# The attention output product written beside the scores, behind the products with v, and another order of VectorE's work in a round

## The reference

```python
qkv = x @ Wqkv.T + bqkv                      # x: the layernorm of the input
scores = einsum('bhid,bhjd->bhij', q, k) / sqrt(8)
mask = (j <= i) & (j >= i - 31)
probs = softmax(where(mask, scores, -inf))
y = einsum('bhij,bhjd->bhid', probs, v)
out = y @ Wo.T + bo                          # added to the input
```

## Time and profile before

| | us |
|---|---|
| median of 3 runs (2181.7 to 2184.13) | 2182.03 |
| the profiled execution | 2180.72 |
| its span, first to last instruction | 2178.9 |
| TensorE's matmuls busy in the span | 2027.5 |
| VectorE busy | 1491.8 |
| GpSimd busy | 1439.8 |
| ScalarE busy | 1192.3 |

### The profile page before, as it was taken

The page is one execution under the profiler, slowest core; times in us unless marked ns, Lnnn a source line. Parts: engine busy times, 40 slices in busy tenths (PEclk is TensorE's granted clock), DMA queues, the critical chain, the costliest instruction groups (busy, mean ns, idle before and its releaser), DMA issues. The chain is left out here.

```text
span 2178.9 us, 42631 instructions
## 1 busy us (share of the span) xinstructions
PE 2027.5 (93%) x14462; PEld 1546.1 (71%) x14463; DVE 1491.8 (68%) x2745; ACT 1192.3 (55%) x2383; POOL 1439.8 (66%) x972
## 2 busy tenths in 40 slices
PE   7998999999999988889998888898779999999998
PEld 5776546999999635556665555665554489999994
DVE  6777585333333479999999999999975833333335
ACT  5665323222222269999999988989833232222222
POOL 6775003777767339999999998989940057777660
PEclk9999999999999999999999999989899999999999
DMA  8000100000000423322232222333233000000004
GB/s 301 1 0 2 39 1 13 26 25 24 25 24 25 114 76 98 99 97 99 101 98 93 96 97 89 99 94 94 89 134 145 0 21 26 25 25 25 24 23 120
DMA packets 72343, 141.93 MB, mean 65 GB/s; under 512 B 9979, under 2 KB 43773, under 8 KB 70054
## 3 DMA queue, kind: packets, MB, share of 16 engines
q1 hardware_dynamic: 63142, 121.87, 17.1%
q0 software_dynamic: 9088, 18.63, 2.9%
HBM read 123.82 MB, written 16.65 MB: 64 GB/s over the span
## 5 line engine op out<-in xcount | busy, mean ns | idle before, releaser
L2205 POOL TENSOR_TENSOR m_seen<-m_state,experts 128x1024 f32<-128x1024 f32 x256 | 599.7, 2365 | 58.8 <-DVE m_state L2259 52.2
L2259 DVE TENSOR_TENSOR_SCAN m_state<-experts,ps 128x512 f32<-128x512 f32 x448 | 540.3, 1235 | 1.4 <-PE ps L1796 1.1
L1813 PE MATMUL ps<-ident,m_seen 128*128 128x128 f32 x2048 | 280.0, 282 | 36.9 <-POOL m_seen L2205 36.9
L1813 PEld LDWEIGHTS ps<-ident,m_seen 128*128 128x128 f32 x2048 | 243.7, 145 | 76.0 <-POOL m_seen L2205 56.1
L2018 ACT ACTIVATE experts<-delta,experts 128x512 f32<-128x512 f32 x448 | 291.3, 713 | 1.0 <-DVE delta L2285 0.5
L1527 POOL COPY f_weights<-experts 128x1898 f32 x142 | 252.3, 1777 | 23.9 <-issue 23.5
L1350 PE MATMUL first_up_ps<-f_xT,f_weights 128*128 128x128 f32 x1988 | 241.5, 275 | 1.5 <-issue 1.4
L1350 PE MATMUL ps<-zu,f_weights 128*128 128x128 f32 x1988 | 241.5, 275 | 1.5 <-issue 1.4
L1350 PEld LDWEIGHTS first_up_ps<-f_xT,f_weights 128*128 128x128 f32 x1988 | 233.2, 192 | 2.6 <-issue 2.6
L1350 PEld LDWEIGHTS ps<-zu,f_weights 128*128 128x128 f32 x1988 | 233.2, 192 | 2.6 <-issue 2.6
L2239 DVE TENSOR_TENSOR ps<-m_delta_u,ps 128x512 f32<-128x512 f32 x286 | 193.2, 676 | 12.6 <-PE ps L1771 11.9
(11 more groups left out here) (421 smaller groups left out, 3919.2 us busy)
## 6 DMA issues: line engine op xcount, KB each, us to landing
experts<-m_rows SPq DMA_DIRECT2D x144, 512.0 KB, 3.7
experts<-in_experts SPq DMA_DIRECT2D x17, 1461.0 KB, 18.6
tokens<-f_rows SPq DMA_DIRECT2D x8, 512.0 KB, 4.4
f_rows<-expert_out SPq DMA_DIRECT2D x8, 512.0 KB, 7.0
f_cols<-expert_out SPq DMA_DIRECT2D x8, 512.0 KB, 7.3
out<-X SPq DMA_DIRECT2D x4, 512.0 KB, 3.2
X<-in_x SPq DMA_DIRECT2D x4, 448.0 KB, 6.1
f_xin<-tokens,f_take POOLq DMA_INDIRECT x71
```

The source lines that it names most:

```text
L1813: mm = pe.matmul(Y[:, i // 2, at:at + P], seen[:, n % SEEN, h, i * P:(i + 1) * P], ident[:], is_transpose=True, start=(n == 0 and at == 0) ...
L2205: pool.tensor_tensor(seen[:, n % SEEN], state[:, n % RING], c_rep[:, Q % C_RING, n % C_GROUP, :].unsqueeze(1).to_broadcast([P, HALF, SEG]) ...
L2259: dve.tensor_tensor_scan(state[:, n % RING, h, :], decay_, drive_, before_, ALU.mult, ALU.add).then_inc(s_state, 1)
```

## The change

- The output product is written to `beside_scores`: columns 256 to 383 of the second of the four score banks, one block of 128 columns, and no longer to strips of `y_ps`. `add_out` reads it there. In `tail` both stay as they were.
- On TensorE the output product (t-2) moves behind both halves of the products with v (t-1). It gets a wait for the mask of tile t+1 (`s_mask` at its own tile plus 4), since the mask reads the same bank. The second half no longer waits for `s_x`.
- On VectorE a round is now: mask and maxima (t+1), add (t-2), reciprocals and picking (t-1), statistics (t-2), copy of the turned y (t-1).

The diff, without the lines of `tail`, in which only the argument is written out:

```diff
@@ -306,6 +306,7 @@
                 other_y_ps = first_up_ps[:, 2:4, :].rearrange("p a (h c) -> p (a h) c", c=P)
                 turned_in = lambda ps: ps[:, 0:NG, PAIR_END:PAIR_END + 32]
                 summed_in = lambda ps: ps[:, NG:2 * NG, PAIR_END:PAIR_END + 32]
+                beside_scores = first_up_ps[:, 1, HG * KW:HG * KW + D].rearrange("p (k c) -> p k c", k=NG)
                 qkv_ps = scope.enter_context(nc.psum_tensor("qkv_ps", [P, NG, P], F32))
                 v_ps = qkv_ps[:, 2:4, :].rearrange("p a c -> p (a c)")
@@ -529,12 +530,12 @@
                         sums(range(1, 2))
                         variances(dve, s_stats, s_var, second_round, 2)
                         dve.wait_ge(small_in, SMALL)
-                        def add_out(t, j, ps):
+                        def add_out(t, j, summed):
                             dve.wait_ge(s_wo, t + 1)
                             dve.wait_ge(s_biased, t + 1)
                             x = X[:, ds(j * D, D)].rearrange("p (k c) -> p k c", k=NG)
-                            dve.tensor_tensor(x, x, summed_in(ps), ALU.add).then_inc(s_x, 1)
+                            dve.tensor_tensor(x, x, summed, ALU.add).then_inc(s_x, 1)
                         def sums_of(t, j):
@@ -573,16 +574,16 @@
                             dve.tensor_copy(yT[:].rearrange("p (k c) -> p k c", k=NG), turned_in(ps)).then_inc(s_yT, 1)
                         def body(n, r):
-                            if alive(n, r - 2):
-                                add_out(at(n, r - 2), tile(n, r - 2)[0], y_ps)
                             if alive(n, r + 1):
                                 add_mask(at(n, r + 1), (r + 1) % 2)
+                                tops(at(n, r + 1), (r + 1) % 2)
+                            if alive(n, r - 2):
+                                add_out(at(n, r - 2), tile(n, r - 2)[0], beside_scores)
+                            if alive(n, r - 1):
+                                pick(at(n, r - 1), y_ps)
                             if alive(n, r - 2):
                                 sums_of(at(n, r - 2), tile(n, r - 2)[0])
-                            if alive(n, r + 1):
-                                tops(at(n, r + 1), (r + 1) % 2)
                             if alive(n, r - 1):
-                                pick(at(n, r - 1), y_ps)
                                 copy_y(at(n, r - 1), y_ps)
                             if isinstance(n, int) and n == TPB - 2 and r == 0:
                                 variances(dve, s_stats, s_var, FIRST_TILES, 4, NT + B * (GROUP - 1) + 1)
...
@@ -652,18 +653,18 @@
                         def body(n, r):
                             if alive(n, r + 1) and not (isinstance(n, int) and at(n, r + 1) == 0):
                                 scores(n, r + 1)
-                            if alive(n, r - 2):
-                                t = at(n, r - 2)
-                                pe.wait_ge(s_yT, t + 1)
-                                pe.matmul(summed_in(y_ps), yT[:], woT[:], start=True, stop=True).then_inc(s_wo, 1)
                             if alive(n, r - 1):
                                 t = at(n, r - 1)
                                 wait(pe, s_yT, t)
                                 pe.wait_ge(s_turned, 2 * t + 1)
                                 products(r - 1, 0)
-                                wait(pe, s_x, t)
                                 pe.wait_ge(s_turned, 2 * t + 2)
                                 products(r - 1, 1).then_inc(s_pv, 1)
+                            if alive(n, r - 2):
+                                t = at(n, r - 2)
+                                pe.wait_ge(s_yT, t + 1)
+                                pe.wait_ge(s_mask, t + 4)
+                                pe.matmul(beside_scores, yT[:], woT[:], start=True, stop=True).then_inc(s_wo, 1)
                             if alive(n, r + 3):
                                 t = at(n, r + 3)
                                 pe.wait_ge(s_ln, t + 1)
```

More of the change, by code:

```diff
@@ L597, in tail @@
                             j = lambda t: t % B * TPB + TPB - 1
-                            add_out(NEXT - 2, j(NEXT - 2), y_ps)
+                            add_out(NEXT - 2, j(NEXT - 2), summed_in(y_ps))
                             add_mask(LAST, LAST % 2)
@@ L603, in tail @@
                             copy_y(NEXT - 1, y_ps)
-                            add_out(NEXT - 1, j(NEXT - 1), y_ps)
+                            add_out(NEXT - 1, j(NEXT - 1), summed_in(y_ps))
                             sums_of(NEXT - 1, j(NEXT - 1))
@@ L607, in tail @@
                             copy_y(NEXT, other_y_ps)
-                            add_out(NEXT, j(NEXT), other_y_ps)
+                            add_out(NEXT, j(NEXT), summed_in(other_y_ps))
                             sums_of(NEXT, j(NEXT))
@@ L612, in tail @@
                             copy_y(LAST, y_ps)
-                            add_out(LAST, j(LAST), y_ps)
+                            add_out(LAST, j(LAST), summed_in(y_ps))
                             sums_of(LAST, j(LAST))
```

## The result

| | us |
|---|---|
| changed kernel, median of 6 runs (2166.8 to 2173.64) | 2168.37 |
| kernel before, median of 6 runs beside it (2179.36 to 2184.33) | 2181.86 |
| ratio, 95% interval | 0.9941 [0.9927, 0.9955] |
| profiled execution of the changed kernel | 2173.64 |
| its span (before: 2178.9) | 2171.9 |

The change is 0.6% faster. On 2181 us the four ratios are gains of 12.9, 12.2, 9.6 and 9.4 us. The forecast was 10.3 us; its time, 2171.7, lies 3.3 us above the median of the first six runs, and the range, which ended at 2169.0, left that median out by 0.6 us.

A forecast was written before the change was run, and what follows sets the result against it. Attention was taken as bound by TensorE and VectorE waiting for each other each round; rounds falling to 5.42 us gain 8.8 in the loop and 1.5 outside, so 2182.0 - 10.3 = 2171.7 us, range 2169 to 2178.

The forecast's parts named there:

- What bounded the kernel: Attention: VectorE waits 25.0 us for the output product, TensorE 9.5 us for the picked y, once each round.
- The order on VectorE: Mask needs only the scores, starting 0.88 us after them; maxima follow directly; statistics between picking and copy cost nothing.
- The ring: Attention round from one turned y to the next, through scores, mask, maxima, add, reciprocal and picking: 5.35 us, before 5.86.
- rival (a): Mask starts 1.17 us after the scores, as in the cold round: round 5.64, gain 4.9, time 2177.1 us; chance 0.17.
- The order on TensorE: TensorE's own round without waiting for y: 0.23 + 2.70 + 1.91 + 0.57 = 5.41 us in the loop, 5.48 allowed outside.
- The added wait: Output product on TensorE waits for the mask sharing its bank; hidden with 0.24 us to spare.
- The add's cover: VectorE's add needs the output product at 3.36 us and is reached at 3.48, so its wait is hidden by 0.12.
- The sum: Attention rounds become 5.42 us: 20 loop rounds gain 8.8, six others 1.5, total 10.3 us.
- (b): TensorE's idle time before the turned y is partly its own dispatch; rounds shrink 0.1 only, 2.6 us, 2179.4; chance 0.12.
- (c): The mask's wait holds TensorE's output product and the queue behind it; slower, about 2187 us; chance 0.05.
- The range: Whole program from 2169 to 2178 us; chance 0.80 faster, 0.15 within 0.2%, 0.05 slower.
- 12.0 us: Most TensorE can give back in attention: 9.5 us of waits for y plus 28 times 0.09; leads to 2170.0.

The follow-up runs named there:

- the four ratios: Four comparisons of the unedited changed kernel with the kernel before: 0.9941, 0.9944, 0.9956 and 0.9957.
- the fourth execution: Changed kernel, unedited, timed and profiled a fourth time; ratio to the kernel before 0.9957, median 2170.63 us.
- The late add: Changed kernel with the output product back in strips of y_ps and the add moved behind the picking; 0.9943 (2165.58 us), second time 0.9934 (2164.04 us).
- add early: Changed kernel with the add moved between mask and maxima; one run, 2193.98 us.
- the kernel with the statistics ahead: Changed kernel with the statistics moved from behind the picking to between add and reciprocal; ratio to the kernel before 1.0006, median 2182.26 us.
- the old place: Changed kernel with both new orders, but the output product back in strips of y_ps and no wait for the mask; ratio 0.9927, median 2166.93 us.
- the changed kernel's second: Changed kernel, unedited, timed and profiled a second time; ratio to the kernel before 0.9944, median 2167.98 us.

## Why the prediction was right, and where it was not

**What bounded the kernel.** Right. The two waits of the earlier trace rows went away together, and nothing of their size took their place.

**The order on VectorE.** The ring was forecast at 5.35 and is 5.40 in the rows at 100.38 to 105.78: scores 0.23, mask 0.90 (forecast 0.88), maxima 1.26 (1.26), add 1.14 (1.11), reciprocal 0.19 (0.20), picking 0.29 and 1.24 (the same), turn of y 0.15 (0.14). The late mask of rival (a), 1.17, did not come: warm, the mask follows the scores by 0.90. Statistics at no cost: right, the copy starts 0.34 after the turned y as before (105.78 to 106.12; 105.62 to 105.96).

**The order on TensorE.** Forecast 5.41, in truth 5.35. The failing term is the 0.57 from the second turn of the probabilities to y. I called the row at 32.78 one without a wait because the view prints no idle time there. But VectorE's timeline of the kernel before has this row ahead of it:

```profile
31.39 1.24 DVE L566 TENSOR_TENSOR y<-y_ps,inv 32x128 f32<-32x128 f32 x4
```

The picking ended at 32.63, and 0.15 later TensorE followed it, as in every other round; VectorE had released it. Unwaited it is 0.49 (100.32 to 100.81). The other errors partly cancel it: from y to the scores 0.20 and not 0.23, but products and output product 1.83 + 0.28 = 2.11 and not 0.32 + 1.73 = 2.05.

So I had the two engines in the wrong order, TensorE at 5.41 above VectorE at 5.35; they are 5.35 and 5.40, in that order. The round, 5.40 for a forecast of 5.42, came out by two small errors of opposite sign; that it fits so well is luck.

**The added wait.** Spare 0.24 forecast; in the rows of the fourth execution the mask at 101.51 ends at 102.73, plus 0.14 is 102.87, and the product starts at 103.10: 0.23. The add's cover was forecast at 0.12: the product at 103.10 plus the 0.65 of the kernel before is 103.75, the add comes at 103.91, 0.16. Both hold in every ordinary round. What I left out are the two rounds with layernorm's statistics, where VectorE is late by about 2 us and any such spare is gone: TensorE idles 2.5 us in them for the mask, of which 0.2 us is the net price.

**The sum.** Loop 8.8 forecast, 8.9 measured. Six rounds outside it 1.5 forecast; measured 1.6 behind the loop and 0.2 ahead of it, since rounds without loop are 5.41 there and not the 5.48 that I had allowed. In all 10.3 against 10.7 by the traces. The forecast let a turn of the loop cost the same before and after, which is not quite so: before, the loop takes 0.43 us a turn more than four rounds of 5.86, after, 0.49 more than four rounds of 5.40. That takes back 0.3 us of what 20 rounds of 0.46 would give, and so the forecast of 0.44 a round comes out nearer than it should. Rivals (b) and (c) are out by the same rows: the round shrank by 0.46, far over the 0.1 of (b), and in an ordinary round the product was not held.

**The range.** This is the step that failed. The medians of the first comparison lie 13.5 us apart, 2.8 more than the traces account for; its interval for the ratio, 9.8 to 15.9 us of gain, holds the 10.7. I took 12.0 us as the most that TensorE could give back and added 1 us for the spread between runs. That spread came from three runs of the kernel before, 2181.7 to 2184.13. Over 12 runs of one comparison the same kernel reaches from 2175.16 to 2185.01, and the baseline of 2182.03 is itself some 1 us high: the medians of 12 to 20 later runs are 2181.69, 2180.9, 2179.97 and 2179.66. The medians of the changed kernel, four times unedited, lie 2.7 us apart, and two of them are below 2169.0 and two above: 2168.37, 2167.98, 2170.39, 2170.63. The mean of all its runs, 2169.7, lies inside the range. A range for a median of six runs has to carry about 2 us on either side of the mechanism's own bounds; 10.3 to 12.0 us of gain with that margin ends near 2168, not at 2169.0.

The 12.0 itself was also too small. It adds to the 9.5 us of waits 28 times the 0.09 that the record of the last turn (0.66) is longer than 0.57. With the unwaited 0.49 it is 28 times 0.17, 14.3 us in all. The late add shows that the 12.0 was no bound: from the scores of tile 5 to the experts its second execution takes 165.7 us where the kernel before took 178.7, 13.1 us less. The changed kernel stayed at 10.7, so this error did not put its time outside the range; the allowance for the spread did.

## What to carry to other kernels

Two engines that wait for each other once a round form a ring; write its length as a sum of distances from start to start, and beside it each engine's own sum, and move out of the ring whatever nobody on it needs (here the add and the statistics, 5.86 to 5.35 at best). An instruction that reads what the one before it wrote starts later than one that does not, so put the reader elsewhere (here a round of 5.82 against 5.40); and a move on one engine can need a move on the other to be any good at all (add early, 6.33 a round). Before a row is called "without a wait", compare its start with the end of what could have released it, since an idle time of zero in the view is no proof; and take the spread of runs from more than three of them.

## What the runs showed of the hardware

**An instruction of VectorE that reads the result of the one ahead.** Add to statistics takes 0.42 us from start to start (103.19 to 103.61; 97.29 to 97.72 in the kernel with the late add), for an add of 0.28 to 0.29. Add to reciprocal, which does not read X, takes 0.19 (103.91 to 104.10). Mask to maxima, which reads `sc`, is 1.26, but maxima to add, for an instruction as long, 1.13 to 1.14. Outside the loop, add to statistics is 0.32 (187.70 to 188.02 in the kernel with the statistics ahead). So 0.12 to 0.13 us go where the next instruction needs the last one's output and waits for its semaphore, and the statistics take 0.10 more inside the loop. No run separates the reading from the wait or from the kinds of instruction.

**The granted clock falls in some executions and not in others.** The changed kernel's first profile, table by stage, 36 to 42 us, the granted clock being the figure behind the five engines:

```profile
36.00:42.00 6.00, 5.27 (x66) 3.78 (x67) 3.90 (x10) 4.26 (x11) 4.29 (x5) 0.72 1.00 420
```

and its fourth profile, the same stretch:

```profile
36.00:42.00 6.00, 5.41 (x79) 4.30 (x79) 5.11 (x12) 4.88 (x13) 4.29 (x5) 1.00 1.02 428
```

In both, TensorE had stood idle for the mask (1.37 us up to 36.73, and 1.42 us up to 36.59); in the first the clock then, from about 38.1 on, went from 2.4 to 1.2 GHz (a mean of 0.72 over 6 us is 3.4 us at one half), in the second it did not. The round took 8.15 there and 7.18 here, 1.0 us more for the fall. The kernel before shows the same: no fall in the attention of its first profile and two in its second, with 8.05 and 7.20 for that round. Of the 13 profiles of all kernels here four had no fall: the first of before, the changed kernel's fourth, the old place and the second of the late add. What decides whether it comes stays open; the idle time ahead of it alone does not, as these two profiles show.

**The start of the attention differs between executions.** From the first scores to those of tile 5 the kernel before took 33.06 us in its first profile and 30.73 in its second; the changed kernel 33.99, 30.67, 30.70 and 32.84. In the longer ones TensorE kept its slower early pace for longer: from the second scores to the third it is 6.54 us in the first profile of before (21.01 to 27.55) and 4.77 in its second (20.03 to 24.80), and the third scores last 0.93 and 0.71; in the loop they last 0.72. The granted clock in the table reads 1.00 there all the same (20 to 28 us of the first profile), so in this stretch the lengths of the matmuls have to be read, not the clock. In the changed kernel's fourth execution the third scores still last 1.16 where they lasted 0.93 in the kernel before, so the 0.2 us of gain ahead of the loop is rather too small.

**Behind the attention** the same code took either about 1950 us (1949.8 to 1950.9, four profiles: the changed kernel's second, add early and both of the late add) or about 1954 (1953.7 to 1955.2, the other nine, among them both of before and three of the changed kernel). The changed kernel shows both, so it is no effect of the change; for the late add two profiles can't say, and the cause stays open. The start, the falls of the clock and this stretch are the differences that the profiles show; single runs of one kernel differ by 10 us from end to end.
